# A graph network kernel: where the product's blocks stand between a slot's counts on TensorE

## The reference

```python
h = jnp.maximum(_layernorm(x, axis=-1), 0.0)
# layer 0: two graph convolutions with symmetric degree scaling (W1, then W2)
    x = x @ W
    norm = dinv[src_f] * dinv[dst_f]
    msg = x[src_f] * norm[:, None]
    out = jax.ops.segment_sum(msg, dst_f, num_segments=n)
...
# layer 1: an edge filter times the gathered row, averaged by destination
    h = jax.nn.silu(edge_attr @ mlp_w1 + mlp_b1)
    W = (h @ mlp_w2 + mlp_b2) * C[:, None]
    msg = xf[src] * W
    agg_sum = jax.ops.segment_sum(msg, dst, num_segments=n_nodes)
```

## The kernel before

| counts | blocks | with two packings | with one | with none |
|---|---|---|---|---|
| 4 | 8 | 18 | 20 | 2 |
| 4 | 9 | 7 | 7 | 0 |
| 4 | 10 | 7 | 9 | 2 |
| 6 | 10 | 4 | 2 | 0 |
| 4 | none | 3 | 5 | 4 |
| 6 | none | 2 | 4 | 0 |

## Time and profile before

### The profile page before, as it was taken

The page is one execution under the profiler, slowest core; times in us unless marked ns, Lnnn a source line. Parts: engine busy times, 40 slices in busy tenths (PEclk is TensorE's granted clock), DMA queues, the critical chain, the costliest instruction groups (busy, mean ns, idle before and its releaser), DMA issues.

```text
span 1469.2 us, 36573 instructions
## 1 busy us (share of the span) xinstructions
PE 1267.0 (86%) x12470; PEld 1097.6 (75%) x12470; DVE 920.2 (63%) x3249; ACT 580.7 (40%) x1265; POOL 1022.6 (70%) x1039
## 2 busy tenths in 40 slices
PE   2357999998998988899589999999999498999996
PEld 2145888787887877788479999999999266776674
DVE  3987576777766776686526556646555535565564
ACT  2947555656656566566113413313310011121121
POOL 7667777776765766576577677777677477777773
PEclk9965999999999999999689999999999588899897
DMA  3246667667666665566768878878867624355432
GB/s 99 80 124 166 182 195 208 189 187 206 199 187 193 181 182 176 147 198 198 229 187 246 261 194 249 251 204 250 250 187 209 152 68 113 84 129 116 117 98 61
DMA packets 260338, 255.28 MB, mean 174 GB/s; under 512 B 136211, under 2 KB 217800, under 8 KB 259253
## 3 DMA queue, kind: packets, MB, share of 16 engines
q1 hardware_dynamic: 217269, 165.00, 38.6%
q0 software_dynamic: 42880, 87.88, 23.1%
HBM read 182.45 MB, written 70.31 MB: 172 GB/s over the span
## 4 chain that ended last, share of the span: by engine, by line
PE 53%; POOL 16%; issue 9%; ACT 6%; DVE 6%; DMA 4%; ACTq 3%; SPq 1%; DVEq 0%; POOLq 0%
PE ps_product L2122 25%; POOL ring_parts L1064 16%; PE ps_pack L2096 9%; PE ps_banks L2078 8%; ACT adjacency L1214 4%; PE ps_banks L2060 3%; ACTq L1244 2%; ACT packed_T L1250 2%; DMA src_raw<-in_src_dram 1%; PE ps_banks L2056 1%; DMA ring_parts<-node_table,packed_src 1%; PE ps_pack L2104 1%; DMA edge_in<-in_edge_attr_dram 1%; PE ps_banks L2166 1%; PE ps_node L2132 1%
## 5 line engine op out<-in xcount | busy, mean ns | idle before, releaser
L2122 PE MATMUL ps_product<-adjacency,table_parts 128*128 128x232 bf16 x4704 | 549.3, 267 | 4.0 <-ACT adjacency L1214 3.2
L1064 POOL DMA_INDIRECT ring_parts<-node_table_parts,src_idx x384 | 385.9, 1005 | 175.5 <-issue 119.8
L1064 POOL DMA_INDIRECT ring_parts<-node_table,src_idx x384 | 378.5, 986 | 153.0 <-issue 112.8
L2122 PEld LDWEIGHTS ps_product<-adjacency,table_parts 128*128 128x128 bf16 x4704 | 461.5, 100 | 20.6 <-issue 8.0
L1214 ACT CAST adjacency<-ps_banks 128x550 f32 x504 | 336.8, 668 | 175.7 <-PE ps_banks L2078 120.5
L2078 PE MATMUL ps_banks<-code_onehot,lo_onehot 128*128 128x400 bf16 (+2 forms) x1494 | 235.3, 269 | 50.6 <-ACT adjacency L1214 46.5
L1064 POOL DMA_INDIRECT ring_parts<-node_table,packed_src x216 | 206.1, 954 | 82.3 <-issue 65.1
L1604 DVE TENSOR_SCALAR code_onehot<-code_iota,code_T 128x600 bf16<-128x600 bf16 x504 | 184.4, 387 | 120.1 <-PE ps_banks L2078 118.7
L1250 ACT COPY packed_T<-ps_pack 67x96 f32 x416 | 97.9, 235 | 366.0 <-PE ps_pack L2096 312.2
L2078 PEld LDWEIGHTS ps_banks<-code_onehot,lo_onehot 128*128 128x128 bf16 x1494 | 148.0, 116 | 101.5 <-issue 49.3
L2096 PE MATMUL ps_pack<-pack_onehot,edge_in 128*67 128x96 f32 x1664 | 173.3, 254 | 14.5 <-ACT packed_T L1250 6.2
(11 more groups left out here) (282 smaller groups left out, 1350.7 us busy)
## 6 DMA issues: line engine op xcount, KB each, us to landing
kept_tiles<-adjacency SPq DMA_DIRECT2D x98, 406.0 KB
adjacency<-kept_tiles SPq DMA_DIRECT2D x98, 406.0 KB, 3.9
edge_in<-in_edge_attr_dram SPq DMA_DIRECT2D x207, 128.0 KB
packed_attr<-packed_T SPq DMA_DIRECT2D x8, 864.0 KB, 7.3
adjacency<-packed_attr SPq DMA_DIRECT2D x6, 1152.0 KB, 9.5
ring_parts<-node_table,src_idx POOLq DMA_INDIRECT x384
ring_parts<-node_table_parts,src_idx POOLq DMA_INDIRECT x384
node_table_parts<-table_parts SPq DMA_DIRECT2D x7, 672.0 KB, 3.7
```

What stands on the lines that cost most here:

```text
L1064: gps.indirect_dma_start(to, None, rows, bass.IndirectOffsetOnAxis(index, 0)).then_inc(gathered[s], 16)
L2122: product = mm(ps_product[:, 0:COLS], table_parts[:, k, part, :], adjacency[:, buffer_of(c, tile), k, :], start=(k == 0 and part == 0), st ...
```

## The change

PE's order in a slot: the blocks are divided into as many even shares as the slot has counts, and one share stands ahead of each count. The packings stand between the second share and the second count. Where a slot has no counts the blocks stay in three shares, with the packings after the first. No other engine's code is touched.

```diff
                     for n in range(SLOT_COUNT[c]):
                         counted = plan.onehots.get(n - 1, [])
-                        half = (len(counted) + 1) // 2
                         pieces = plan.products.get(n, [])
-                        third = len(pieces) // 3
                         packs = plan.packs.get(n, [])
                         if n in plan.ends:
                             turn_packed(plan.ends[n])
                         sum_window(c, n)
-                        for chunk in counted[0:1]:
-                            count_chunk(*chunk)
-                        for piece in pieces[:third]:
-                            multiply(c, *piece)
-                        for q in packs:
-                            pack(q, packs)
-                        for chunk in counted[1:half]:
-                            count_chunk(*chunk)
-                        for piece in pieces[third:2 * third]:
-                            multiply(c, *piece)
-                        for chunk in counted[half:half + 1]:
-                            count_chunk(*chunk)
-                        for piece in pieces[2 * third:]:
-                            multiply(c, *piece)
-                        for chunk in counted[half + 1:]:
-                            count_chunk(*chunk)
+                        for i, share in enumerate(spread(len(pieces), len(counted) or 3)):
+                            for at in share:
+                                multiply(c, *pieces[at])
+                            if i == (1 if counted else 0):
+                                for q in packs:
+                                    pack(q, packs)
+                            if counted:
+                                count_chunk(*counted[i])
                         nodes_at(n)
```

## The result

The changed kernel takes 1495.18 us (median of 4 runs, 1490.96 to 1495.68) where the kernel before takes 1468.9: 1.0194 times as long, 95% interval 1.0168 to 1.0220. In a second series of runs the same pair gave 1493.74 and 1465.94 us, 1.0196 (1.0172 to 1.0221). The profiled execution was the shortest of its four runs, 1490.96 us with a span of 1489.2; that of before was 1471.0. So the two traces show 20 us of a difference whose median is 26.

A forecast was written before the change was run, and what follows sets the result against it. The prediction took TensorE (PE) to set the pace in both passes. Its terms, 21.2 + 2 - 1 - 1 + 0.5 + 3 = +24.7 us, gave a forecast of 1493 us, range 1482 to 1507.

The forecast's parts named there:

- The main step: Pass 1, two-packing slots: ACT copies packings first, so the fourth count starts no earlier than 2.8 us after the second's start.
- T: The start of a slot's second count on PE, right behind the packings; 343.02 in slot 43 of the kernel before.
- lost cover: Pass 1 slots: blocks taken from between the second and fourth counts no longer fill the wait there, +21.2 us in all.
- The first slots of a product: 14 slots of pass 1 whose blocks, waiting for all 28 copies, now precede the first count: +2 us besides other terms.
- the credits: Pass 1: -1 us where packings already waited behind a late first copy, -1 us where blocks cover first counts' waits elsewhere.
- Seven such waits: First blocks of a product in pass 1 waiting for last copies, 3.2 us; with seven other first slots, priced +2 us.
- The credit for packings that wait behind a late first copy: A few first slots of a product: the second count comes 0.6 us later at no cost, -1 us.
- The clock rival: Two-packing slots of pass 1: new gaps lower the clock in 10 to 30 falls, 1510 to 1541 us; chance 0.12.
- +3 us for two more falls: Pass 1, two-packing slots ahead of slots without blocks: two more drops to half clock, 1.6 us each.
- The faster rival: Pass 1: ACT's backlog, not the packings, holds the counts, so blocks ahead help; 1453 us at best, chance 0.05.
- The no-change rival: Pass 1: gathers or DVE's chain take up the new waits, so time stays at 1469 us within 3; chance 0.05.
- Pass 2: Moving blocks costs 0 there, except one run's end where `turn_packed` comes right behind the packing: +0.5 us.

The follow-up runs named there:

- the experiment: The new order everywhere but in the 14 first slots of a product, which keep the old order, against the kernel before: 1481.12 us, ratio 1.0104.

## Why the prediction was right

**The main step held.** "With two packings the fourth count can't start before about T + 2.8": slot 41 shows T + 2.83 before and T + 2.84 after, and the table above has the predicted loss, slot kind by slot kind. For the kinds in it, the prediction's prices come to 12 x 0.60 + 4 x 0.30 + 7 x 0.60 + 18 x 0.21 = 16.4 us, measured 14.5. That ACT's order is the cause of the two-packing slots' waits is shown: with the second copy ahead of the packings, the counts' waits there fall from 22.5 to 4.2 us. That lost cover is the mechanism is shown from two sides: the new order in these slots alone costs 12.1 us, and putting all blocks into the covered stretch makes the kernel faster than before. The counts' waits as a whole grew to 57.6 us in 71 waits, where the prediction had 64 in 80. The idle of the eight-block slots is 0.80 to 0.90 us in 15 of 18, where it had 0.85.

**The first slots of a product were priced too low.** The prediction had +5.9 for the 14, with the credits; the traces show +8.9 in one profile and +12.0 in the second one of the changed kernel (with 45 us of these slots at the lower clock instead of 33, which can make up to 6 of the 12.0), and the experiment some 13. The step that was mis-sized is "Seven such waits, 3.2 us in all, become some 1.5 us longer, and the seven others cost at most the same: +2". The waits became 6.9 us longer. Of the 8.9 us, the lost cover that the prediction counted with the other slots makes 4.9 by its prices, so this step and the credit have cost 4.0 together, where they were priced at +1. Seven slots had shown no wait for ACT before. In five of them (30, 43, 63, 76, 89) the window sum and the first count ran at the lower clock, and this slow work covered the wait. In the changed kernel the fall comes later or not at all in four of the five, and the first block waits 0.70 to 0.99 us there. That this is the reason is read from the traces; no kernel was run for it. The credit for packings that wait behind a late first copy was real: in slot 50 the fourth count started 3.28 us behind T before and 2.76 after.

**The clock rival** did not come. The mean granted clock of pass 1 is 0.96 in both traces and 0.95 in the second profile of the changed kernel, with an idle of 0.5 to 1.2 us in 31 of the 32 slots with two packings. What became of the prediction's +3 us for two more falls (6.4 us at half speed) is not settled. Pass 1 has 45 us at the lower level before and 44 in the changed kernel, but 58 in its second profile. In the second series the mean granted clock of the whole execution is 0.918 in the five runs of the changed kernel and 0.922 in the 23 of the kernel before. By the granted clocks and the spans that is 245 and 228 us at the lower level, an estimate; 17 us more cost 9 us at most, and less where PE waits anyway. The Trainium skill (TensorE: Matmul & The Clock Gate, section A second HAM failure mode: psum-queue depth-cycling) describes a clock that swings under frequent short idle spells; these traces agree only in part. Of the falls of pass 1 up to the end of its counts, 11 of 13 in the kernel before and 8 of 10 and 11 of 13 in the two profiles of the changed one begin in a slot without blocks, where several waits stand close together, or in the slot behind it. None begins in one of the other slots with two packings, which have one long wait.

**The faster rival** did not come. It was nearly right about the place: ACT's queue does hold the counts, but by what stands in it (the packings' copies), not by a backlog. In slot 41 of the changed kernel ACT was idle for 1.89 us before it took up the packings' result, and the swap on ACT removed the wait. The advice of the Trainium skill (Perfetto Trace Analysis, section Optimization Strategy) to find the semaphore a gap waits on and the instruction that updates it is what tells the two apart: the copy was late because of its place in ACT's queue, and even shares on PE do nothing to that.

**The no-change rival** fell: POOL's wait for window sums grew from 55.7 to 82.3 us (20 more were predicted), so the gathers followed PE and did not pace it.

**Pass 2** kept its length to 1 us, and in the kernel with the new order there alone the time is 2 us above, within what can't be told from none.

**The sum**: 24.7 us was predicted; the medians differ by 26.3, in the second series by 27.8, and the two profiled executions by 20. The parts that missed had opposite signs: the first slots +3 to +7 more, the other priced slots -1.9, and the clock anything from -3 to +6. So it is in part luck that the sum came within 2 to 3 us. Two of the prediction's sums have a slip that changes nothing: 18 x 0.60 is 10.8, not 10.7, and 17.0 less twice the credits of 2 is 13, not 14.

## What to carry to other kernels

Work that covers a wait is worth its time only at the place where the wait is: before spreading it evenly, measure from which event the limit counts (here the packings' end: the fourth count is released 2.8 us behind it with two of them and about 2.0 with one), and put as much work as fills it behind that event. Look for that event in the other engine's queue order; a count waited for a copy that could have been made some 1.5 us earlier but stood behind copies that nobody needed yet. And when a queue is reordered, price the wait of whoever needs what is now last.

## What the runs showed of the hardware

The same slot can run at different granted clocks from one kernel to the next, and where it does, this moves its length more than the change does. Slot 57, the kernel before and then the changed one:

```profile
415.50:424.20 8.70, 7.74 (x69) 6.59 (x68) 4.63 (x17) 3.68 (x9) 6.73 (x7) 0.80 0.78 225
```

```profile
430.30:438.00 7.70, 6.02 (x74) 5.43 (x71) 4.78 (x17) 3.64 (x9) 6.18 (x6) 1.00 0.79 235
```

And slot 89, before and after:

```profile
620.50:626.10 5.60, 5.45 (x60) 4.69 (x57) 4.86 (x18) 3.03 (x7) 3.57 (x4) 0.90 0.69 206
```

```profile
637.70:646.30 8.60, 7.79 (x64) 6.38 (x61) 5.31 (x18) 3.42 (x8) 3.92 (x4) 0.60 0.68 228
```

Slot 57 lost its fall of the clock and got 1.0 us shorter with 0.3 us less cover; slot 89 got 3.0 us longer. Over pass 1 these shifts nearly cancel in this pair of traces (44 and 45 us at the lower level), but not in the second profile of the changed kernel (58 us). A single slot, or a single run, is a poor measure of a change of this size: the profiled execution of the changed kernel lies 4 us under its median.
